# Storing gathered rows unchanged, adding the constant vector by an accumulating transfer, and taking the rows' low parts ahead of the sums

## The reference

```python
h = take(W.T, x, axis=0)                       # one gathered row of 256 per token
n = layernorm(h)
f = layernorm(mamba(n, ..._f), ln_g_f, ln_b_f)             # forward scan, 512 inner, 32 states
b = layernorm(mamba(n[:, ::-1], ..._b)[:, ::-1], ln_g_b, ln_b_b)
h = h + concat([f, b]) @ Wfuse.T + bfuse       # the rows called h_rows (h1) below
h = h + ffn(layernorm(h))                      # attention, router, 8 experts
```

## Time and profile before

| | us |
|---|---|
| time, median of 3 runs | 4073.57 (4070.09 to 4075.94) |
| profiled execution, its own time | 4076.19 |
| its span, first to last instruction | 4074.6 |
| one sequence in the middle of the scan (two slots) | 71.69 |

### The profile page before, as it was taken

The page is one execution under the profiler, slowest core; times in us unless marked ns, Lnnn a source line. Parts: engine busy times, 40 slices in busy tenths (PEclk is TensorE's granted clock), DMA queues, the critical chain, the costliest instruction groups (busy, mean ns, idle before and its releaser), DMA issues. The chain is left out here.

```text
span 4074.6 us, 70440 instructions
## 1 busy us (share of the span) xinstructions
PE 3755.3 (92%) x19212; PEld 2734.8 (67%) x19213; DVE 3416.2 (84%) x6582; ACT 2950.8 (72%) x4862; POOL 2410.6 (59%) x2145
## 2 busy tenths in 40 slices
PE   5999999999999999999999969999999699999998
PEld 3655666566565665656565547777777588888887
DVE  6998989999898998989999849998998566666665
ACT  5788888888888888888888857777776344444444
POOL 3555555555556555555555556777777455555555
PEclk8999999999999999999999979999999799999999
DMA  3333444333444333444433422222222455555555
GB/s 86 65 78 72 81 81 81 75 68 77 79 81 80 73 79 66 81 81 81 76 72 78 72 60 89 92 98 86 97 92 82 137 95 96 97 95 95 84 96 85
DMA packets 216894, 339.70 MB, mean 83 GB/s; under 512 B 25425, under 2 KB 145106, under 8 KB 216786
## 3 DMA queue, kind: packets, MB, share of 16 engines
q0 software_dynamic: 112864, 197.71, 27.8%
q1 hardware_dynamic: 100480, 138.48, 12.1%
q10 hardware_dynamic: 3442, 2.21, 0.2%
HBM read 121.07 MB, written 150.14 MB: 67 GB/s over the span
## 5 line engine op out<-in xcount | busy, mean ns | idle before, releaser
L644 PE MATMUL pj<-xt,win 128*128 128x512 f32 x3144 | 896.7, 439 | 143.6 <-DVE xt L824 123.3
L644 PEld LDWEIGHTS pj<-xt,win 128*128 128x128 f32 x3144 | 632.5, 207 | 357.4 <-DVE xt L824 124.8
L2040 POOL DMA_INDIRECT out<-e_y,e_to x272 | 469.3, 1725 | 369.5 <-ACT e_y L2146 309.5
L325 POOL TENSOR_TENSOR wk<-v,uc 128x512 f32<-128x512 f32 x260 | 325.7, 1287 | 505.7 <-DVE v L885 505.7
L837 DVE SCALAR_TENSOR_TENSOR uc<-pj,convw,uc 128x511 f32<-128x511 f32 (+2 forms) x780 | 516.8, 728 | 5.7 <-ACT uc L423 5.7
L693 PE MATMUL po<-yz,wout 128*128 128x512 f32 x1024 | 472.8, 604 | 21.7 <-ACT fb L513 21.7
L2091 PE MATMUL e_p<-e_w,e_a 128*128 128x256 f32 x3264 | 416.3, 284 | 1.2 <-DVE e_a L2201 1.2
L2091 PEld LDWEIGHTS e_p<-e_w,e_a 128*128 128x128 f32 x3264 | 393.7, 188 | 11.6 <-DVE e_a L2201 2.9
L2079 PE MATMUL e_p<-e_xt,e_w 128*128 128x512 f32 x1632 | 395.2, 397 | 4.0 <-DVE e_xt L2193 2.4
L693 PEld LDWEIGHTS po<-yz,wout 128*128 128x128 f32 x1024 | 184.2, 190 | 256.6 <-issue 255.9
L2079 PEld LDWEIGHTS e_p<-e_xt,e_w 128*128 128x128 f32 x1632 | 303.3, 189 | 74.8 <-issue 5.8
(11 more groups left out here) (244 smaller groups left out, 8565.6 us busy)
## 6 DMA issues: line engine op xcount, KB each, us to landing
qq<-uc POOLq DMA_DIRECT2D x128, 512.0 KB, 5.6
e_x<-expert_in SPq DMA_DIRECT2D x138, 260.0 KB, 2.6
bb<-bc SPq DMA_DIRECT2D x65, 512.0 KB, 4.9
h_rows<-fb POOLq DMA_DIRECT2D x64, 512.0 KB, 9.6
h_rows<-h0c SPq DMA_DIRECT2D x32, 512.0 KB, 5.5
a_h<-h_rows SPq DMA_DIRECT2D x128, 128.0 KB
out<-a_bs SPq DMA_DIRECT2D x128, 128.0 KB
bc<-xd SPq DMA_DIRECT2D x65, 128.0 KB, 7.3
```

Of the source, the lines that this page charges most:

```text
L325: pool.tensor_tensor(wk[:, m, :], v[:, m, :], uc[d][:, m, :], ALU.mult).then_inc(S["dtu_ok"], 1)
L644: i = mm(pj[m][:], win[d][wp][:, k, c:c + P], xt[xp][:, k, :], start=(k == 0 and n == 0), stop=(k == KD - 1 and n == 2))
L2040: pool.indirect_dma_start(out=out, out_offset=bass.IndirectOffsetOnAxis(ap=to[n][:, j:j + 1].bitcast(U32), axis=0), in_=y[n][:, j, :], in_ ...
```

## The change

`h0c`, `keep_residual` and the semaphore `h0_ok` go. SP stores `g` as it was gathered (`store_rows`), when the gather has landed, one sequence further ahead than before: two stores ahead of `broadcast(0, 0)`, then `store_rows(s + 2)` where `store_residual(s + 1)` was. POOL adds `cvec` to the stored rows in DRAM by an accumulating transfer from a broadcast source (`add_bias`), in the place of `keep_residual`; it waits for the store of that sequence (`h1_st`), no longer for `outputs`. `add_rows` waits for `add_bias` of its sequence, the next gather for the store of `g`. At the start `gather(1)` comes ahead of `add_bias(0)`. Two sequences more are stored than are used, so `h1_rows` has 34 x 512 rows. On DVE `xt_low` moves ahead of `sums`.

```diff
-            def store_residual(s):
-                sp.wait_ge(S["h0_ok"], s + 1)
+            def store_rows(s):
+                wait_apart(sp, S["gath"], 16 * TT * (s + 1))
                 dst = h1_dram[bass.ds(s * SEQ, SEQ), :].rearrange("(j p) c -> p j c", p=P)
-                sp.dma_start(dst, h0c[:, bass.ds(s % 2, 1)].squeeze(1)).then_inc(S["h1_st"], 16)
+                sp.dma_start(dst, g[:]).then_inc(S["h1_st"], 16)
...
-            store_residual(0)
+            store_rows(0)
+            store_rows(1)
             broadcast(0, 0)
...
                     if d == 1:
-                        store_residual(s + 1)
+                        store_rows(s + 2)
...
                     pool.wait_ge(S["xn_ok"], TT * s)
-                    pool.wait_ge(S["h0_ok"], s)
+                    pool.wait_ge(S["h1_st"], 16 * s)
...
-            def keep_residual(s):
-                if not (isinstance(s, int) and s < 2):
-                    pool.wait_ge(S["h1_st"], 16 * (s - 1))
-                pool.wait_ge(S["prep_v"], 3 * DIRS + 2)
-                pool.wait_ge(S["gath"], 16 * TT * (s + 1))
-                pool.tensor_tensor(h0c[:, bass.ds(s % 2, 1)].squeeze(1), g[:],
-                                   cvec[:].unsqueeze(1).to_broadcast([P, TT, DM]), ALU.add).then_inc(S["h0_ok"], 1)
+            def add_bias(s):
+
+                wait_apart(pool, S["prep_v"], 3 * DIRS + 2)
+                wait_apart(pool, S["h1_st"], 16 * (s + 1))
+                pool.wait_ge(S["c_tab"], 1)
+                dst = h1_dram[bass.ds(s * SEQ, SEQ), :].rearrange("(j p) c -> p j c", p=P)
+                pool.dma_start(dst, cvec[:].unsqueeze(1).to_broadcast([P, TT, DM]), accum_op=ALU.add
+                               ).then_inc(S["bias"], 16)
...
-                wait_apart(pool, S["h1_st"], 16 * (s + 1))
+                wait_apart(pool, S["bias"], 16 * (s + 1))
...
             ln_scale(0)
-            keep_residual(0)
             gather(1)
+            add_bias(0)
             ln_scale(1)
...
                     if d == 0:
-                        pool.wait_ge(S["hc_ok"], t + 1)
-                        keep_residual(s + 1)
+                        add_bias(s + 1)
...
                     more_states(t, d)
-                    sums(t)
                     if d == 0:
                         xt_low(s + 1)
+                    sums(t)
                     gate(t, d)
```

More of the change, by code:

```diff
@@ L107, in mamba_stage @@
         xt = [sb(f"xt{h}", [P, KD, SEQ], F32R) for h in range(2)]
-        h0c = sb("h0c", [P, 2, TT, DM])
         fb = [sb(f"fb{i}", [P, TT, DM]) for i in range(2)]
@@ L143, in mamba_stage @@
         names = """c_tab cv xl_ok ld_win0 ld_win1 ld_w0 ld_w1 ld_ids prep_a win_ok split
-          rows_ok prep_w prep_v idc_ok gath st_ok lnv_ok lnr_ok xn_ok xt_ps xt_ok h0_ok
+          rows_ok prep_w prep_v idc_ok gath bias st_ok lnv_ok lnr_ok xn_ok xt_ps xt_ok
           u_ps a_ok z_ps z_ok uc_ok xd_ps xd_ok bc_ok bcast xd_st dt_ps v_ok vc_ok y_ok l_ok w_ok g_ok
@@ L238, in slots @@
                     if d == 1:
-                        store_residual(s + 1)
+                        store_rows(s + 2)
             slots(0)
-            with sp.Fori(1, NSEQ - 1) as s:
+            with sp.Fori(1, NSEQ) as s:
                 slots(s)
[L244 to L248, removed]
+            sp.wait_ge(S["h1_st"], 16 * (NSEQ + 2))
             sp.wait_ge(S["bcast"], 16 * (2 * NSEQ + 1))
@@ L374, in _ @@
             pool.wait_ge(S["acc"], 16 * DIRS * NSEQ)
+            pool.wait_ge(S["bias"], 16 * (NSEQ + 1))
             pool.wait_ge(S["gath"], 16 * TT * (NSEQ + 2))
@@ L2227, in build @@
 def build(nc, h, out):
-    h1_dram = nc.dram_tensor("h1_rows", [NSEQ * SEQ, DM], F32).ap()
+    h1_dram = nc.dram_tensor("h1_rows", [(NSEQ + 2) * SEQ, DM], F32).ap()
     xd_dram = nc.dram_tensor("expert_in", [NE * X_ROWS, XW], F32).ap()
@@ L2247, in build @@
             w2=[[sb(f"e_w2{i}{h}", [P, MF, DM], F32R) for h in range(2)] for i in range(2)])
-        attention_stage(nc, h, h1_dram, out, xd_dram, moe)
+        attention_stage(nc, h, h1_dram[0:NSEQ * SEQ, :], out, xd_dram, moe)
         expert_stage(nc, h["moe_w1"], h["moe_w2"], h["ln2"], xd_dram, out, moe)
```

## The result

The changed kernel takes 3887.19 us (median of 4 runs, 3885.86 to 3887.42) against 4071.83 us for the kernel before on the same chip: a ratio of 0.9545, with a 95% interval of 0.9533 to 0.9557. The profiled execution took 3887.42 us, its span is 3885.9 us. Lines have moved up by three or four: DVE's L945, L824, L854, L885 and L892 are now L942, L821, L851, L882 and L889; POOL's L281, L301, L325 and L331 are L277, L297, L322 and L328; PE's L644 is L641; `add_bias` is L305.

A forecast was written before the change was run, and what follows sets the result against it. DVE was taken as the bound, PE close behind, with about 6 us lost in slot d = 0. 31 x 6.19 + 3.1 + 4.8 = 199.8 us off 4076.2 leaves 3876.4; the median is 2.6 lower: 3874, range 3858 to 3930.

The forecast's parts named there:

- rival B: POOL late: gather issues beside DVE's softplus lengthen, POOL loses 4.9 to 9.8 us; total 3896 to 4048; chance 0.08.
- xt_low ahead of the sums: DVE, slot d = 0: xt_low goes first, with a new uncovered wait of about 0.75 us for ACT's copy.
- PE: PE, slot d = 0: the 3.76 us pause goes, the clock stays 1.00, the input product takes 3.01 us.
- Rival E: PE's clock stays low: input product still at 0.50, taking 5.49 us; total 3945; chance 0.06.
- POOL's add: POOL's 3.25 us add of cvec goes, and its hold on DVE's L945, 2.17 us per sequence; pair takes 2.36.
- D: The hold on L945 stays, being caused by DMA traffic; L885 comes 2.17 us later; total 3941; chance 0.03.
- Slot d = 0: The sequence's first slot, L885 to L885: 38.96 us falls by 6.19, to 32.5 to 33 us.
- add_bias: POOL's added accumulating transfer: issue of 1.33 us hidden in POOL's idle time, landing after 9.6 us.
- rival C: Added transfer delays bb for L331: decides from 16.0 us of added delay; 4153 at 25; chance 0.03.
- POOL's room: POOL may lose 0.4 + 3.8 = 4.2 us before DVE's scan lacks a product and DVE feels it.
- The rule set against it there: POOL writes transfer descriptors into SBUF; DVE's two-port modes lock it out, so gather issues beside softplus would lengthen.
- Start and first sequence: Gather(1) no longer waits for cvec: 4.8 us gained at the start (0 to 6.1); first sequence 3.1 (0 to 6.2).

The follow-up runs named there:

- the spare instructions: Changed kernel with one small unused POOL pow of about 1.05 us behind each slot d = 0 gather, 3920.96 us; with three, 3981.06 us.
- the transfer alone: Changed kernel with DVE's xt_low behind sums again, as before, keeping the accumulating transfer: 3961.89 us, ratio 0.9727.
- The order alone: Kernel before with xt_low ahead of sums on DVE, POOL still adding the constant vector in SBUF: 3910.50 us, ratio 0.9602.
- the gather moved forward: Changed kernel with POOL's gather ahead of its row_scale in slot d = 0: 3869.56 us, ratio 0.9504.

## Why the prediction was right, and where it was off

The time was forecast at 3874 with 3858 to 3930; 3887 came, inside the forecast's own 3866 to 3897 too. That it stayed so near has some luck in it: the cause that it had set down as rival B came in part, at half of B's least size (2.5 us on POOL for 4.9). At the one us for each us of lateness that the spare instructions cost, B's 4.9 us would have cost 2.4 us more per sequence, by my estimate 3961. By its steps:

- **xt_low ahead of the sums: right.** The new wait is 0.77 us for 0.75, the L942 pair starts 1.20 us behind the start of L821, as set down.
- **PE: right.** No pause, 3.00 us for the product at a clock of 1.00, `dead_test` waits for nothing. Rival E did not come; but the transfer alone shows how near it lay: there the product behind 1.59 us of pause took half as long again.
- **POOL's add: right.** The hold is gone, 2.35 us for 2.36; D fell. The order alone shows the same hold from the other side: where the add ran beside another step, L945 lost 0.6 us.
- **Slot d = 0** was forecast at 32.77 and took 32.66 us.
- **add_bias: right that it is hidden, low in the landing.** The issue holds POOL for 1.31 us, forecast 1.33. It landed 12.2 us after its start (median), against the 9.6 taken from fb's; `bb` landed at 5.7 instead of 4.9, a delay far from the 16 us at which rival C decides. The scan without it ends about 1 us earlier.
- **POOL's room: this step failed.** The prediction gave POOL 0.4 us until v is ready and 3.8 us until a scan would lack its input, and so took rival B's price as starting at 4.2 us. Two things were wrong. The four gather issues did lengthen, by 2.5 us, though L319 beside the scans had shown nothing of the kind: that row was of another kind of issue, beside another DVE instruction. The rule set against it there gave the right sign, but no run shows that `softplus` runs in the modes that the rule names. Other terms gave some of it back: `row_scale` took 1.11 us and not the 1.87 set down, the copy of the list 0.32 instead of 0.91, so POOL came 0.85 us behind v and not 2. And the room was counted to the first product that is needed, where it ends when the last product ends after the scan is due: before, that was 0.1 us. DVE lost 0.54 us in each of 31 sequences, 17 us. One spare instruction cost as much as its length, three cost nearly as much as theirs, the gather moved forward gave 17.6 us back.
- **Start and first sequence: right in kind.** 6.0 for 4.8 and 3.7 for 3.1 us, the 3.1 being no more than the middle of its bounds. I had put the start down to the order of the gather alone; that is 3.4 of it, and the other 2.5 came with the add gone from POOL, in part unexplained.
- The sum was 199.8, and 188.7 came: about 16 less by POOL's room (31 x 0.53 in slot d = 1), 3 more by the 31 slots d = 0, 2 more at the start and in the first sequence.

## What to carry to other kernels

Ask of every pair of instructions on VectorE and GpSimd not only when the one needs the other's result, but whether they would run at the same time on SBUF: a queue of GpSimd products that ended after VectorE's scan, a step with two inputs in SBUF, was due cost that step nearly all of the overlap here, ready data or not. When a wait is removed, look at what used to stand beside it: GpSimd's gather issues were short before because VectorE was idle beside three of the four. And a step that feeds TensorE belongs ahead of a longer one whose result is wanted later; that order of two steps was worth 163 us here by itself, because it also spared TensorE the pause of 3.76 us behind which its clock was 0.50.

## What the runs showed of the hardware

**GpSimd's products shut VectorE's scan out as a block.** With four products queued, the scan that was due behind the first waited for the end of the fourth: 4.69 us for a scan of 1.19. In the kernel before, the other order: POOL's add (3.25 us, where it takes 2.38 beside `xt_low`) waited for a running half of L945, and the next half then for the add. VectorE's steps with one input in PSUM did not wait so: in the same run the convolution (7.95 us) ended and `dead_part` (2.46 us) went through while the products were running. The Trainium skill, page "SBUF — State Buffer", section "SBUF: two separate sides", calls the pair of ports that the two share an exclusive lock: whichever instruction starts first has it to its end, and the other is blocked fully. The runs agree, and add that a queue of GpSimd instructions keeps it from one to the next.

**A transfer issue of GpSimd can be held up by VectorE, depending on the instruction.** The long issues end a nearly fixed time after a DVE instruction. DVE's timeline beside the gather in the changed kernel:

```profile
952.56 1.23 DVE L874 SCALAR_TENSOR_TENSOR wk<-wk,lg 128x1024 f32<-128x1024 f32 x1
...
954.97 1.22 DVE L874 SCALAR_TENSOR_TENSOR wk<-wk,lg 128x1024 f32<-128x1024 f32 x1
...
957.68 2.27 DVE L882 SCALAR_TENSOR_TENSOR v<-v,wk 128x2048 f32<-128x2048 f32 x1
```

These end at 953.79, 956.19 and 959.95 us; the issues that began beside them at 953.26, 955.10 and 958.60 end at 954.79, 957.05 and 960.78, 0.8 to 1.0 us behind, about the length of an issue that stands alone (0.94 us). In these rows an issue is longer by about what is left of that DVE instruction when it begins; in the transfer part alone two began 0.25 and 0.13 us before such an end, took 1.08 and 0.95 us, and ended 0.8 us behind it. Beside the scan of slot d = 0 L316 took 1.31 us, no more than with DVE idle at the end of the scan stage (1.32). One difference is that the gather issue L277 reads its list of rows (`idc`) in SBUF, and L316 has no such list. With the gather first the same happens beside L904 and the L942 pair, whose inputs are both in SBUF too: an issue of 2.15 us ends 0.9 us behind L904. The same section of the Trainium skill's page "SBUF — State Buffer" says that a VectorE instruction with two SBUF inputs excludes only a GpSimd instruction that reads SBUF; that would fit both cases. In the middle of the scan stage no gather issue begins beside a scan in any of these runs, so whether it is the issue's kind or VectorE's stays open.
